# The ternary feed-forward stage's last three tiles in another order, the last tile's y in buffers of its own

## What is computed

```python
qb = float(2 ** (bits - 1))                                    # act_quant, bits = 8
scale = qb / jnp.clip(jnp.max(jnp.abs(x), axis=-1, keepdims=True), EPS)
xq = jnp.clip(jnp.round(x * scale), -qb, qb - 1) / scale
...
scale = 1.0 / jnp.clip(jnp.mean(jnp.abs(w)), EPS)              # weight_quant
wq = jnp.clip(jnp.round(w * scale), -1.0, 1.0) / scale
...
gate = bitlinear(x, w_gate)
up = bitlinear(x, w_up)
intermediate = jax.nn.silu(gate) * up
return h_bitlinear(intermediate, w_down)       # Hadamard transform over 2048, quantized, times w_down
...
x = _layernorm(x + _L0_ffn_ref(x, L0_ffn_w_gate, L0_ffn_w_up, L0_ffn_w_down), axis=-1)
```

## Time and profile before

| | us |
|---|---|
| Time, median of three executions | 1797.99 |
| lowest and highest | 1797.62, 1799.31 |
| The profiled execution: its time | 1797.66 |
| its span | 1795.8 |

### The profile page before, as it was taken

The page is one execution under the profiler, slowest core; times in us unless marked ns, Lnnn a source line. Parts: engine busy times, 40 slices in busy tenths (PEclk is TensorE's granted clock), DMA queues, the critical chain, the costliest instruction groups (busy, mean ns, idle before and its releaser), DMA issues. The chain is left out here.

```text
span 1795.8 us, 26361 instructions
## 1 busy us (share of the span) xinstructions
PE 1602.3 (89%) x8780; PEld 1128.4 (63%) x8812; DVE 1299.9 (72%) x2362; ACT 937.0 (52%) x1932; POOL 682.0 (38%) x638
## 2 busy tenths in 40 slices
PE   7999998999866999986699989999888989999995
PEld 5788875555424665655466666566557767677774
DVE  6466756666778999995567486684849999866674
ACT  3221236776665656654356366474644555554552
POOL 5034256677422333230232132231322225565563
PEclk9999999999987999998999999999999999999998
DMA  6200028433020000000512112121313100000000
GB/s 211 71 16 9 1 87 219 152 108 95 12 84 1 1 1 1 1 1 24 148 53 70 46 49 69 37 79 46 102 44 117 51 30 1 1 24 0 24 24 24
DMA packets 66849, 95.71 MB, mean 53 GB/s; under 512 B 12177, under 2 KB 28689, under 8 KB 66717
## 3 DMA queue, kind: packets, MB, share of 16 engines
q1 hardware_dynamic: 58460, 80.40, 14.6%
q0 software_dynamic: 6144, 12.60, 2.6%
q10 hardware_dynamic: 2112, 1.05, 0.2%
HBM read 56.25 MB, written 4.19 MB: 34 GB/s over the span
## 5 line engine op out<-in xcount | busy, mean ns | idle before, releaser
L2753 PE MATMUL bank<-fp_xT,fp_weights_values 128*128 128x512 f32 x704 | 187.3, 404 | 11.4 <-DVE fp_gate L2656 9.7
L1568 ACT ACTIVATE causal_probs<-bank,causal_neg 128x512 f32<-128x512 f32 (+3 forms) x256 | 134.1, 530 | 114.8 <-DVE causal_neg L1660 74.6
L2753 PEld LDWEIGHTS bank<-fp_xT,fp_weights_values 128*128 128x128 f32 x704 | 129.9, 190 | 56.8 <-DVE fp_gate L2656 18.0
L2780 PE MATMUL bank<-fp_wd,fp_hT 128*128 128x512 f32 x528 | 133.8, 394 | 4.6 <-DVE X L2678 3.4
L1458 POOL DMA_DIRECT2D causal_qS<-causal_qk x96 | 48.0, 507 | 227.6 <-DVE causal_qk L1618 227.4
L2665 DVE SCALAR_TENSOR_TENSOR fp_up<-bank,fp_weights_scales,fp_up 128x512 f32<-128x512 f32 x132 | 99.1, 751 | 44.7 <-ACT fp_up L2563 35.7
L820 DVE TENSOR_REDUCE heads_neg<-bank 128x1 f32<-128x512 f32 x128 | 86.7, 680 | 58.1 <-PE bank L869 58.0
L782 ACT ACTIVATE heads_probs<-bank,heads_neg 128x512 f32<-128x512 f32 x128 | 88.1, 689 | 77.5 <-DVE heads_neg L820 77.5
L2780 PEld LDWEIGHTS bank<-fp_wd,fp_hT 128*128 128x128 f32 x528 | 98.5, 188 | 29.0 <-issue 6.6
L1032 POOL TENSOR_TENSOR ternary_z<-ternary_z 128x1024 f32<-128x1024 f32 x16 | 37.6, 2353 | 205.8 <-DVE ternary_z L1160 205.8
L1810 PE MATMUL bank<-causal_kS,causal_qS 96*128 96x512 f32 (+3 forms) x256 | 84.4, 382 | 27.4 <-ACT causal_probs L1568 18.1
(11 more groups left out here) (256 smaller groups left out, 4127.6 us busy)
## 6 DMA issues: line engine op xcount, KB each, us to landing
pairs_xd<-X SPq DMA_DIRECT2D x64, 128.0 KB, 2.6
pairs_cd<-in_ctx SPq DMA_DIRECT2D x64, 128.0 KB, 2.7
causal_qS<-causal_qk SPq DMA_DIRECT2D x96, 64.0 KB, 2.8
causal_qS<-causal_qk POOLq DMA_DIRECT2D x96, 64.0 KB, 2.5
causal_kS<-causal_qk SPq DMA_DIRECT2D x96, 64.0 KB, 2.8
causal_kS<-causal_qk POOLq DMA_DIRECT2D x96, 64.0 KB, 2.5
X<-in_x SPq DMA_DIRECT2D x4, 1024.0 KB, 7.5
heads_cT<-in_ctxT SPq DMA_DIRECT2D x4, 1024.0 KB, 6.2
```

The lines of the kernel that those rows point to most:

```text
L1568: act.activation(probs_of(i)[:, h + one], view[:, one], ACT.Exp, bias=neg[:, G % 2, at:at + 1], accum_out=total[:, G % 2, at:at + 1]).then ...
L2753: last = pe.matmul(banks[4 + g][:], values[:, g, n % NI, of], xT[:, part, g], start=part == 0, stop=part == 1)
L2780: last = pe.matmul(banks[t][:], hT[:, n % SLOTS, a, t * P:(t + 1) * P], wd[:, c, i], start=i == 0 and k == 0, stop=i == NI - 1 and k == 2)
```

## The change

`LAST` is 15, the last tile. The loops end after step 15, and the rest is written out on each engine. Three things differ:

- TensorE: the down products of tile 13 stand before the Hadamard products of tile 14; tile 15 is turned and multiplied straight after tile 14, before y of tile 14 is turned.
- ScalarE and VectorE follow: ScalarE copies the turned z of tile 15 before it scales y of tile 14; VectorE clips y of tile 15 before it adds tile 14's down products to `X`.
- Tile 15's y is kept in `z2[:, 0]` and its turned form in the space of `z2[:, 1]`, both free by then, so they do not wait for tile 14's y and yT to be used up. No memory is added.

The number of instructions on each engine stays the same, and so do their sizes.

```diff
@@ -1036,14 +1036,27 @@
             return 0 <= t < TILES
 
 
+
+        LAST = TILES - 1
+        y_of = lambda t: z2[:, 0] if t == LAST else y[:]
+        yT_last = z2[:, 1].bitcast(BF16)[:, 0:FF].rearrange("p (a n) -> p a n", n=P)
+        yT_of = lambda t: yT_last if t == LAST else yT[:]
+
+
         order = []
-        for t in range(-1, TILES + 4):
-            if tile(t - 3):
-                order += [("yT", t - 3, g) for g in range(2)]
-            if tile(t - 2):
-                order += [("zT", t - 2, g) for g in range(CH)] + [("y", t - 2, c) for c in range(CH)]
-            if tile(t + 1):
-                order.append(("qT", t + 1, 0))
+
+        def uses(kind, t):
+            if tile(t):
+                order.extend((kind, t, i) for i in range({"yT": 2, "zT": CH, "y": CH, "qT": 1}[kind]))
+
+        for t in range(-1, TILES):
+            uses("yT", t - 3)
+            uses("zT", t - 2)
+            uses("y", t - 2)
+            uses("qT", t + 1)
+        for kind, t in (("yT", LAST - 2), ("zT", LAST - 1), ("y", LAST - 1), ("zT", LAST), ("y", LAST), ("yT", LAST - 1),
+                        ("yT", LAST)):
+            uses(kind, t)
...
-            for t in range(TILES + 4):
+            for t in range(TILES + 3):
...
+            def keep_yT(t):
+                if not tile(t):
+                    return
+                for g in range(2):
+                    act.wait_ge(y_turned, 2 * t + g + 1)
+                    if 0 < t < LAST:
+                        act.wait_ge(down_ready, t)
+                    act.activation(yT_of(t)[:, 8 * g:8 * g + 8].rearrange("p a n -> p (a n)"),
+                                   bank("yT", t, g)[:].bitcast(BF16), ACT.Copy).then_inc(yT_ready, 1)
+
+            def keep_zT(t):
+                if not tile(t):
+                    return
+                for g in range(CH):
+                    act.wait_ge(z_turned, CH * t + g + 1)
+                    if t:
+                        act.wait_ge(y_ready, CH * t)
+                    act.activation(zT[:, 4 * g:4 * g + 4].rearrange("p a n -> p (a n)"), bank("zT", t, g)[:],
+                                   ACT.Copy).then_inc(zT_ready, 1)
+
+            def keep_y(t):
+                if not tile(t):
+                    return
+                for c in range(CH):
+                    act.wait_ge(y_ready, CH * t + c + 1)
+                    if 0 < t < LAST:
+                        act.wait_ge(yq_ready, t)
+                    act.activation(y_of(t)[:, c * D:(c + 1) * D], bank("y", t, c)[:], ACT.Copy).then_inc(y_kept, 1)
+
+            def shift_y(t):
+                if not tile(t):
+                    return
+                act.wait_ge(y_rated, t + 1)
+                act.activation(y_of(t), y_of(t), ACT.Copy, scale=rate_y[:, t % NT:t % NT + 1], bias=ROUND).then_inc(y_shifted, 1)
+
...
-            for t in range(-1, TILES + 4):
...
+                shift_y(t - 2)
+
+            for t in range(-1, TILES):
                 step(t)
+            keep_yT(LAST - 2)
+            keep_zT(LAST - 1)
+            keep_y(LAST - 1)
+            keep_zT(LAST)
+            shift_y(LAST - 1)
+            keep_y(LAST)
+            keep_yT(LAST - 1)
+            shift_y(LAST)
+            keep_yT(LAST)
 
...
-                dve.tensor_reduce(peak_y[:, i], y[:], AX, ALU.max, apply_absolute_value=True).then_inc(y_peaked, 1)
+                dve.tensor_reduce(peak_y[:, i], y_of(t), AX, ALU.max, apply_absolute_value=True).then_inc(y_peaked, 1)
...
+            def add_down(t):
+                if not tile(t):
+                    return
+                dve.wait_ge(down_ready, t + 1)
+                x = norm.tile(0, t)
+                dve.scalar_tensor_tensor(out=x, in0=banks[4][:], scalar=down_step[:, t % NT:t % NT + 1], in1=x,
+                                         op0=ALU.mult, op1=ALU.add).then_inc(norm.summed, 1)
+
+            def round_y(t):
+                if not tile(t):
+                    return
+                dve.wait_ge(y_shifted, t + 1)
+                if t:
+                    dve.wait_ge(y_turned, 2 * t)
+
+                dve.tensor_scalar(yq[:], y_of(t), ROUND + QB - 1, ROUND, ALU.min, ALU.subtract).then_inc(yq_ready, 1)
 
...
-            for t in range(-1, TILES + 4):
+            for t in range(-1, TILES):
                 step(t)
+            for n in range(3):
+                butterfly_stage(LAST, n)
+            peaks(LAST - 1)
+            add_down(LAST - 2)
+            norm.statistics(dve, 0, LAST - 2)
+            round_y(LAST - 1)
+            norm.scale(dve, 0, LAST - 2)
+            peaks(LAST)
+            round_y(LAST)
+            for t in (LAST - 1, LAST):
+                add_down(t)
+                norm.statistics(dve, 0, t)
+                norm.scale(dve, 0, t)
 
...
+            def down(t):
+                if not tile(t):
+                    return
+                if t == 0:
+                    pe.wait_ge(weights.measured, 2)
+                    pe.wait_ge(weights.kept, 12)
+                else:
+                    pe.wait_ge(norm.summed, t)
+                for g in range(2):
+                    pe.wait_ge(yT_ready, 2 * t + g + 1)
+                    for a in range(8 * g, 8 * g + 8):
+                        last = pe.matmul(banks[4][:], yT_of(t)[:, a], w_down[:, a], start=a == 0, stop=a == NA - 1)
+                last.then_inc(down_ready, 1)
+
...
                 gate_up(t, 0)
                 gate_up(t, 1)
+                turn_y(t - 3)
+                turn_z(t - 2)
                 gate_up(t, 2)
...
+                products(t - 2)
                 gate_up(t, 3)
...
+                down(t - 3)
...
-            for t in range(-1, TILES + 4):
+            for t in range(-1, TILES):
                 step(t)
+            turn_y(LAST - 2)
+            turn_z(LAST - 1)
+            down(LAST - 2)
+            products(LAST - 1)
+            turn_z(LAST)
+            products(LAST)
+            turn_y(LAST - 1)
+            down(LAST - 1)
+            turn_y(LAST)
+            down(LAST)
 
```

More of the change, by code:

```diff
@@ L1100, in step @@
                 silus(t, 1)
[L1101 to L1114, removed]
-                silus(t, 2)
[L1116 to L1121, removed]
+                keep_yT(t - 3)
+                keep_zT(t - 2)
+                silus(t, 2)
+                keep_y(t - 2)
                 silus(t, 3)
@@ L1262, in gate_up, with turn_y, turn_z, products @@
                     last.then_inc(ready, 1)
+            def turn_y(t):
+                if not tile(t):
+                    return
+                pe.wait_ge(yq_ready, t + 1)
+                for g in range(2):
+                    to = take("yT", t, g).bitcast(BF16)
+                    for a in range(8):
+                        last = pe.transpose(to[:, a * P:(a + 1) * P], yq[:, (8 * g + a) * P:(8 * g + a + 1) * P], eye16[:])
+                    last.then_inc(y_turned, 1)
+            def turn_z(t):
+                if not tile(t):
+                    return
+                pe.wait_ge(butterfly, 3 * (t + 1))
+                for g in range(CH):
+                    to = take("zT", t, g)
+                    for k in range(4):
+                        last = pe.transpose(to[:, k * P:(k + 1) * P], z2[:, t % 2, (4 * g + k) * P:(4 * g + k + 1) * P], ident)
+                    last.then_inc(z_turned, 1)
+            def products(t):
+                if not tile(t):
+                    return
+                for c in range(CH):
+                    pe.wait_ge(zT_ready, CH * t + c + 1)
+                    to = take("y", t, c)
+                    for k in range(4):
+                        last = pe.matmul(to[:, k * P:(k + 1) * P], zT[:, 4 * c + k], had[:], start=True, stop=True)
+                    last.then_inc(y_ready, 1)
+            def down(t):
+                if not tile(t):
+                    return
+                if t == 0:
[3 more added lines that the diff above has]
+                    pe.wait_ge(norm.summed, t)
+                for g in range(2):
+                    pe.wait_ge(yT_ready, 2 * t + g + 1)
+                    for a in range(8 * g, 8 * g + 8):
+                        last = pe.matmul(banks[4][:], yT_of(t)[:, a], w_down[:, a], start=a == 0, stop=a == NA - 1)
+                last.then_inc(down_ready, 1)
             def step(t):
@@ L1285, in step @@
                               stop=True).then_inc(weights.spread, 1)
-                if tile(t - 2):
-                    for c in range(CH):
-                        pe.wait_ge(zT_ready, CH * (t - 2) + c + 1)
-                        to = take("y", t - 2, c)
-                        for k in range(4):
-                            last = pe.matmul(to[:, k * P:(k + 1) * P], zT[:, 4 * c + k], had[:], start=True, stop=True)
-                        last.then_inc(y_ready, 1)
+                products(t - 2)
                 gate_up(t, 3)
@@ L1295, in step @@
                     start.turn_q(pe, t + 1, take("qT", t + 1, 0))
```

(16 more changed lines are left out.)

31 lines of the change are left out of this document (2 added, 29 removed).

## The result

| | us |
|---|---|
| Changed kernel, median of nine executions | 1792.43 (1791.02 to 1794.62) |
| Kernel before, median of nine, the three above among them | 1796.7 (1794.53 to 1799.31) |
| Ratio, changed over before | 0.9979, 95% interval 0.9969 to 0.9989 |
| Profiled execution of the changed kernel: time, span | 1791.02, 1789.2 |

The kernel is faster by 4.3 us by the medians, 3.8 us by the ratio. 1792.1 us was forecast. The time was met closely, the gain less so: 5.9 us was forecast. The kernel before had a median of 1797.99 in the three executions that the prediction started from and 1796.7 in nine. So the close match of the time is in part luck: the starting time was 1.3 us too high and the forecast gain 1.6 us too large, and the two errors nearly cancel.

A forecast was written before the change was run, and what follows sets the result against it. The ternary stage's uncovered tail was taken to bound the kernel: 4.1 us from tile 15's earlier search plus 1.7 us from the clock gave 5.8 us, hence 1792.1 us; forecast 1791 to 1793.3 (52%), 8-in-10 range 1789.9 to 1795.3.

The forecast's parts named there:

- What bounds the kernel: Ternary stage's tail: an uncovered chain; the causal stage starts after its last addition, so each microsecond off its end counts.
- the second rival: Causal stage: its first transposes and a second set of products fall to 1.2 GHz, paying back gain: 1795.7 us; 10%.
- extra gain: Causal stage, the other way round: its first eight products also at full clock, gaining another 1.7 to 1.9 us: 1790.3; 10%.
- Step 1: TensorE: tile 13's down products before tile 14's Hadamard products take 3.5 us; a loss of 3.7 us for tile 14's chain.
- Steps 2 to 4: Tile 14's products, copies, search and scaling, to 822.6; tile 15's fourth Hadamard chunk waits about 1.0 us for ScalarE.
- Step 5: VectorE: the search for tile 15 starts at 824.9 instead of 829.02, a gain of 4.1 us.
- Steps 6 and 7: Tile 15 from search to turned y: last down products start at 833.0; bank 4 is free at 831.9, 1.1 us ahead.
- Step 8: TensorE's shorter idle times keep its clock up; the last down products take 3.6 instead of 5.30 us, gaining 1.7 us.
- that rival: TensorE's clock falls all the same in the idle times before the last down products: 1793.9 us; 20%.
- The sum: Whole tail: last addition starts at 836.6 instead of 842.43, 5.8 us earlier; forecast median 1792.1 us, ratio 1.0033.
- The rule on bank waits: Small idle times between matmul groups cycling PSUM banks can swing TensorE's clock; by it the gain would be 4.1 us.
- Slower and no change: Slower: clock stays low through the tail, 1801 us, 4%. No change: an unseen wait, such as bank 4, undoes it, 4%.

The follow-up runs named there:

- products_first: Changed kernel with tile 13's down products left behind the Hadamard products of tile 14, as before the change: 1789.85 us, ratio 0.9959 over the kernel before.
- old_buffers: Changed kernel with tile 15's y and its turned form back in the old buffers: 1793.87 us, ratio 0.9981 over the kernel before.
- before_filled: Kernel before, old order and buffers, with unused matmuls in TensorE's idle times in the tail (15 in each of three, 3 in one): 1794.92 us, ratio 0.9988.
- changed_all_filled: Changed kernel with 15, 6 and 3 unused matmuls ahead of turning y of tile 13, turning y of tile 15 and its down products: 1790.68 us, ratio 0.9963.
- products_first_filled: Changed kernel with tile 13's down products behind tile 14's Hadamard products, and 15, 6 and 3 unused matmuls in idle times: 1790.04 us, ratio 0.9961.
- changed_again: Changed kernel run again without edit, with a second profile: 1792.71 us, ratio 0.9976 over the kernel before.
- before_again: Kernel before run again without edit, for a second profile: 1797.15 us, ratio 1.0002 over the kernel before in the same series.

## Why the prediction came out

- **What bounds the kernel.** Right. The first load of the causal stage moved with the last addition, and the causal stage took about the same time as before to its first score (24.88 and 24.32 us, before 24.83 and 24.98). The pay-back of the second rival did not come. Of its extra gain, 1.7 to 1.9 us, nothing came in the first profile and about 0.5 us in the second.
- **Step 1** (tile 13's down products first, 3.5 us on tile 14's chain). Right in size: 807.04 to 810.49. By the working it reaches the last tile only through the wait that step 4 named, about 1.0 us: `products_first` put it at 1.1 to 1.3 us and its filled pair at 1.0. The prediction had the move on tile 14's chain as a loss but did not ask what the change would be without it.
- **Steps 2 to 4.** Products to last copy took 4.37 us (4.45 forecast), copy to scaling 2.93 (2.9), and the new wait was 1.52 us (about 1.0). It was longer because TensorE reached it sooner than I had added up: three chunks were done 8.4 us after tile 14's Hadamard products began, not 9.0 (turning z took 2.00 us and not 2.2, and began 0.3 us sooner). The search's start is set by ScalarE and not by this: it came 11.72 us after the same mark, 11.7 forecast.
- **Step 5.** The search of tile 15 was to start 824.9 - 804.36 = 20.5 us after the mark; it started 822.21 - 802.73 = 19.5 us and, in the second profile, 20.5 us after it. Most of the first profile's 1.1 us is the clock, which was low for fewer of the rows at 803 to 807 (1.43 and 3.25 us instead of 1.89 and 3.62).
- **Steps 6 and 7.** Search to the last down products took 8.05 us (8.1 forecast); bank 4 was free at 829.0, 1.2 us ahead.
- **Step 8** (the clock stays up, 1.7 us). This is the weak step: it failed in a part of the executions. Of the four profiles with tile 15 moved ahead and no fillers (`products_first` and `old_buffers` among them), the last down products took 5.30 and 5.14 us in two and 3.61 us in two. I had given that rival 20%; by these four it is about even. So its worth is nearer half of 1.7 us. In all four profiles with fillers ahead of them, one of each kernel, they took 3.4 to 3.6 us, with the clock at 1.00. The step's list of idle times also lacked the one ahead of tile 14's down products, 0.80 us.
- **The sum.** The forecast tail was 836.6 - 804.36 = 32.2 us; 32.87 and 32.20 were measured. Two errors met in the time. The baseline was too high: a median of three executions, 1.3 us above the one of nine. And the gain was mis-sized, 5.8 us by the marks where the medians gave 4.3 (4.1 in the second series). Of its two terms, the schedule (steps 1 to 7, 4.1 us) held: 3.8 us in the tail and 4.2 us in time between the old order and the changed kernel, both filled, where the whole tail is at full clock. The clock (step 8, 1.7 us) is the term that was too large. By the mean of two profiles each, the tail became 5.2 us shorter (37.7 to 32.5), which leaves about 1.4 us for the clock; in the medians almost nothing is left for it. The 0.9 us between 5.2 and 4.3 lies within the interval of the ratio, and nothing in the profiles accounts for it. It stays open.
- **The rule on bank waits.** With the clock at 1.00, waits of 0.22 to 0.26 us between groups of transposes recur in `before_filled`, `changed_all_filled` and `products_first_filled`, and the clock did not fall. The rule in the Trainium skill ("TensorE: Matmul & The Clock Gate", "A second HAM failure mode: psum-queue depth-cycling") was not borne out for waits of this size between transposes of 128 columns. The fall that did come followed idle times of 1.58 and 0.76 us with 1.07 us of turning between them. In `changed_again` and `old_buffers` it did not come after the same two idle times; what decides between the two is not shown.
- **Slower and no change.** Neither came; the clock was back at 1.00 at 807 in the first profile and at 811 in the second.

## What to carry to other kernels

When a pipeline drains, look for an engine that waits with ready work of a later tile queued behind the waiting instruction, and move that work ahead; then check which other moves of the same edit sit on the last tile's chain, and measure each alone. Here one of them (tile 13's down products first) cost 1.0 to 1.3 us of what the others gained. Take the baseline from more than one profile when the gain is a few microseconds and TensorE's clock changes level inside the stretch.

## What I had not expected of the hardware

The same program met the low clock in different places: in two profiles of the kernel before, the turning of tile 13's y took 1.89 and 1.07 us and the last down products 5.30 and 5.65 us. The ten times of `before_again` ran from 1794.69 to 1799.27 us, and times went with the mean granted clock of the whole execution: of the 23 executions of the kernel before in that series, the 8 with a clock of 0.970 or more took 1795.6 us on average and the 15 with a lower one 1797.8 us. That the clock makes the whole difference is not shown.

And TensorE's clock could be held by work without use: 3 to 15 matmuls of 128x512 in idle times of 0.8 to 3.5 us took all low-clock rows out of a stretch, for 3.0 to 3.7 us of the tail in the kernel before, and delayed no other engine. In the tails of all profiles, the clock fell during 9 of the 11 idle times of 3.4 to 3.5 us that were left open or within 2 us behind them, and at none of the 5 that were filled. With one profile of each filled kernel, that fillers always hold it is not shown.
